# Router logits from four column tiles, and the second sum over states moved ahead of them

## The chip, the cores and the metric

The kernel runs on one NeuronCore of a Trainium2 chip. The metric is the device time of one execution in microseconds; a lower time is better. The time before is the median of three runs, the profile is of a fourth execution.

## The reference, cut to what matters

The reference is one transformer-like layer on x of shape (4, 2048, 256): an adaLN-modulated Mamba block (selective scan), then an adaLN-modulated mixture of experts with 8 experts, of which one is shared and one of the other seven is chosen for each token.

```python
h = layernorm(x) * (1 + ca) + sa
x = x + ga * mamba(h)          # in_proj, conv of 4 taps, silu, x_proj, dt_proj, softplus,
                               # scan of 16 states over 2048 steps, * silu(res), out_proj
h = layernorm(x) * (1 + cb) + sb
x = x + gb * moe(h)

def moe(x_MD):                 # D = 256, H = 512, N = 8 experts, the last one shared
    s_raw_MN = x_MD @ Wg_DN    # the router's logits: (8192, 256) @ (256, 8)
    routed = softmax(s_raw_MN[:, :7])
    sel = routed * one_hot(top_1(routed))
    gates = [sel / sum(sel), softmax(s_raw_MN[:, 7:])]
    for each expert: y += g[:, None] * ((silu(bgate) * a) @ w2),  a, bgate = split(x_MD @ w1)
```

## The kernel before

The 8192 tokens are worked through as 16 chunks of 512 (T); four chunks make one batch row, after which the scan's state starts anew. All data is float32. The 512 channels times 16 states of the scan are cut into 16 sets (NSET): set s holds 32 channels, and its tile in the ring `hs` has 128 partitions (32 channels by 4 groups of states) by 4 (NG) states by 512 steps. The ring has 8 slots.

For each set the engines do this. ScalarE makes dA with four exponentials, one for each of the set's four scans, into three PSUM banks (L843, `exps`; exponential number u waits for scan u-3). VectorE multiplies u by B into the ring (L954, `states_in`) for ten of the sets, GpSimd for the other six (L1258), and VectorE does four scans per set (L967, `scan_set`). ScalarE saves the last state of each set (L863, `save`); GpSimd waits for that and multiplies the set by C (L1265, `weigh_states`). TensorE sums four sets over the states with `sum_states` (L585), four matmul streams side by side in column tiles of 32; the result y of group j (`SUM`, j) is gated by VectorE (L976). GpSimd's states_in for set 13 waits for the second sum (`y_ready`), since the ring's slot is free only then.

All other work is laid between these steps by tables written out by hand. `plan` lists TensorE's groups of matmuls by set, `evict` and `vector` the steps with which ScalarE and VectorE take their results, by set and by position g after one of the set's four exponentials or scans, `gps` GpSimd's and `transfers` SyncE's. Each engine does its list strictly in order. The second number of an entry is the offset of its chunk: in the body of chunk c the front of chunk c+1 or c+2 is made (`T`, `XS`, `CV`, `RS`, `XP`, `DT`, `DB`), and the back of chunk c-1: `OP` (out_proj), `T2` (transposes of the second norm), `RB` (transposes back into rows, for the store to `token_rows`), `GL` (the router's logits), `A` and `B` (the shared expert's two halves), `Y` (its second matmul).

Results of TensorE that ScalarE takes go alternately to two PSUM banks, in the order of `plan` (`bank_of`: the index among ScalarE's groups modulo 2); those that VectorE takes go to a third. `take_bank` lets a group start only when the bank's former content was taken.

Around the change, in set 9 of `plan`: `GL` multiplies 128 tokens at a time (stationary, 128x128) with the router's weights (moving, 8 columns), for 4 tiles of tokens by 2 halves of D (L550). Then comes `RB` 1 (four transposes, L545), then `SUM` 1 (L585), then `B` 0 to 3 (L556). ScalarE copies the logits into `lg` (L734) in set 10 behind the first exponential, then takes two logarithms (L742) and the transposes (L730); it copies `B` 0 behind the third, `B` 1 behind the fourth exponential of set 10, `B` 2 behind the last of set 11, `B` 3 behind the first of set 12 (L738). Behind the second exponential of set 12 comes `SRS`: a table load, silu of the next chunk's `res` (L750), silu of the shared expert's gate (L754), a table load (L757). VectorE gates `SUM` 1 behind the second scan of set 10. SyncE stores the rows (L385) once `RB` 1 is copied; behind that in its queue are the loads of d_rep for set 12 and later (L365).

A sum over states and the logits as they are:

```python
for n in range(NG):                      # SUM, L583 to L587
    for q in range(SPC):
        last = nc.tensor.matmul(ps_[DS * q:DS * q + DS, :], t["gather"], hs[:, (SPC * j + q) % RING, n, :],
                                start=(n == 0), stop=(n == NG - 1), skip_group_check=True, tile_position=(0, DS * q))
```

When the 16 chunks are done, the tokens are sorted to their experts, and the routed experts run for 70 tiles of tokens, from about 2028 us to the end.

## Time and profile before

| what | value |
|---|---|
| median of three runs | 2469.89 us (2469.07 to 2472.47) |
| the profiled execution's own time | 2472.81 us |
| its span, first to last instruction | 2471.1 us |
| mean granted TensorE clock | 0.905 |
| TensorE busy | 2179.9 us, 88% |
| VectorE busy | 1946.6 us, 79% |
| GpSimd busy | 1981.0 us, 80% |
| ScalarE busy | 1344.0 us, 54% |

The profiled execution took 1.7 us more than its span, and 2.9 us more than the median. In the views, PE is TensorE, PEld its weight loads, DVE VectorE, ACT ScalarE, POOL GpSimd, SPq SyncE's DMA queue. A float32 matmul has two records (two passes) in the trace, a transpose one. The granted clock is given as a share of 2.4 GHz, so 0.5 is 1.2 GHz. "<-" names the instruction that ended an engine's idle time.

### The profile page before, as it was taken

Reading aid. Unit: us, or ns where it says so; the run is one execution under the profiler, and the core shown is the slowest. Engines: PE = TensorE matmul, PEld = TensorE weight load, DVE = VectorE, ACT = ScalarE, POOL = GpSimd, SP = SyncE. Lnnn points to the kernel's source line nnn. Section 1 sums busy time; section 2 is a strip of 40 time slices with the busy share of each in tenths; the row PEclk is TensorE's granted clock in tenths of the full one; section 3 lists DMA queues with packets and bytes.
Section 4 is the critical chain, followed back from the end, with each engine's and each line's share of the span. In section 5 each row is a group of like instructions: output and inputs, shape, how many; then the busy total and the mean of one; then the engine's idle time right before and its main releaser. Section 6 shows DMA issues by size and latency. Waiting matters only on the chain. (4 is left out here: it accounts for less than half of the span.)

```text
span 2471.1 us, 31167 instructions
## 1 busy us (share of the span) xinstructions
PE 2179.9 (88%) x7668; PEld 1057.8 (43%) x7669; DVE 1946.6 (79%) x2106; ACT 1344.0 (54%) x2377; POOL 1981.0 (80%) x858
## 2 busy tenths in 40 slices
PE   8759999989989898989898989998975679999998
PEld 3214343434434343434343444343432455565665
DVE  2799898999999999989999999999999852222222
ACT  3666666666675757576666666666655212222221
POOL 1999898899989898989898989889889554555553
PEclk9868888898989898989898989989887889999999
DMA  5444242424242423333324324342322512222221
GB/s 156 134 112 98 66 99 77 100 67 112 80 100 66 104 71 98 81 98 83 98 70 99 91 74 120 86 101 68 92 71 60 192 51 82 86 85 85 87 85 47
DMA packets 148362, 224.37 MB, mean 91 GB/s; under 512 B 47187, under 2 KB 84577, under 8 KB 144098
## 3 DMA queue, kind: packets, MB, share of 16 engines
q1 hardware_dynamic: 134818, 182.40, 28.2%
q0 software_dynamic: 13376, 40.12, 5.3%
q8 instruction: 57, 0.93, 0.2%
q14 instruction: 111, 0.91, 0.1%
HBM read 99.46 MB, written 31.45 MB: 53 GB/s over the span
## 5 line engine op out<-in xcount | busy, mean ns | idle before, releaser
L1265 POOL TENSOR_TENSOR ring<-ring,reps 128x2048 f32<-128x2048 f32 x256 | 1154.5, 4529 | 41.4 <-ACT state L863 41.3
L967 DVE TENSOR_TENSOR_SCAN ring<-dA,state,ring 128x512 f32<-128x512 f32 x768 | 930.9, 1263 | 20.5 <-ACT dA L843 16.3
L843 ACT ACTIVATE dA<-d_rep,a 128x512 f32<-128x512 f32 x1024 | 689.7, 686 | 426.9 <-DVE ring L967 423.2
L1258 POOL TENSOR_TENSOR ring<-u_rep,reps 128x2048 f32<-128x2048 f32 x96 | 436.3, 4545 | 90.2 <-PE bank L585 90.2
L954 DVE TENSOR_TENSOR ring<-u_ps,reps 128x2048 f32<-128x2048 f32 x160 | 360.7, 2271 | 11.1 <-PE u_ps L575 5.7
L556 PE MATMUL bank<-n,w1s 128*128 128x512 f32 x512 | 268.3, 661 | 63.5 <-DVE delta L935 39.2
L585 PE MATMUL bank<-ring,spread 128*32 128x512 f32 x2048 | 285.2, 707 | 31.3 <-POOL ring L1265 26.8
L967 DVE TENSOR_TENSOR_SCAN ring<-dA,ring 128x512 f32<-128x512 f32 x256 | 294.1, 1201 | 20.7 <-ACT dA L843 19.5
L1539 DVE TENSOR_TENSOR hid<-z,sg 128x512 f32<-128x512 f32 x70 | 48.4, 692 | 293.8 <-ACT sg L1516 293.8
L1454 PE MATMUL z<-ring,hT 128*128 x560 | 260.7, 608 | 3.3 <-issue 1.9
L514 PE MATMUL bank<-xin,w_in 128*128 128x512 f32 x512 | 246.3, 621 | 9.1 <-ACT xin L696 9.1
L518 PE MATMUL bank<-xpad,w_conv 128*128 128x512 f32 x512 | 230.7, 600 | 8.3 <-ACT us L711 8.2
L525 PE MATMUL bank<-xdbl,w_dt 65*128 65x512 f32 x256 | 149.8, 683 | 68.5 <-ACT n L727 50.4
L556 PEld LDWEIGHTS bank<-n,w1s 128*128 128x128 f32 x512 | 97.3, 203 | 209.9 <-issue 105.8
L1421 POOL DMA_INDIRECT out<-outr,cur x70 | 71.0, 1014 | 143.3 <-DVE outr L1532 136.3
L575 PE MATMUL u_ps<-us,spread 32*128 32x512 f32 x320 | 165.0, 719 | 2.5 <-DVE ring L954 2.5
L585 PEld LDWEIGHTS bank<-ring,spread 128*32 128x32 f32 x2048 | 69.5, 127 | 225.6 <-issue 206.3
L514 PEld LDWEIGHTS bank<-xin,w_in 128*128 128x128 f32 x512 | 99.7, 198 | 131.6 <-issue 119.9
L1454 PEld LDWEIGHTS z<-ring,hT 128*128 128x128 f32 x560 | 101.4, 191 | 121.1 <-issue 120.9
L518 PEld LDWEIGHTS bank<-xpad,w_conv 128*128 128x128 f32 x512 | 95.1, 190 | 135.5 <-issue 114.7
L1516 ACT ACTIVATE sg<-z 128x512 f32<-128x512 f32 x70 | 41.8, 597 | 197.5 <-PE z L1454 194.7
L1472 PE MATMUL y_ps<-reps,hidT 128*128 x560 | 132.4, 379 | 0.8 <-ACT hidT L1505 0.8
(232 smaller groups left out, 2538.4 us busy)
## 6 DMA issues: line engine op xcount, KB each, us to landing
d_rep<-delta SPq DMA_DIRECT2D x1024, 64.0 KB, 2.0
reps<-bc_rows SPq DMA_DIRECT2D x128, 256.0 KB, 6.1
u_rep<-us SPq DMA_DIRECT2D x384, 64.0 KB, 2.0
xres<-in_x SPq DMA_DIRECT2D x16, 512.0 KB, 3.6
token_rows<-xpad SPq DMA_DIRECT2D x32, 256.0 KB, 2.3
token_rows<-xres SPq DMA_DIRECT2D x16, 512.0 KB, 2.9
xin<-in_x SPq DMA_DIRECT2D x15, 512.0 KB, 9.5
ring<-in_w SPq DMA_DIRECT2D x7, 1024.0 KB, 14.4
```

The lines of the kernel that those rows point to most:

```text
L514: last = nc.tensor.matmul(ps_[:, :], t["w_in"][:, k, col:col + P], hT[:, k, :], start=(k == 0), stop=(k == KD - 1))
L518: last = nc.tensor.matmul(ps_[:, :], t["w_conv"][:, j, k, :], xpad[:, j, k:k + T], start=(k == 0), stop=(k == KCONV - 1))
L525: last = nc.tensor.matmul(ps_[:, :], t["w_dt"][:, j * P:(j + 1) * P], xdbl[0:DT_ROWS, :], start=True, stop=True)
L556: last = nc.tensor.matmul(ps_[:, :], t["w1s"][:, k, col:col + P], h2T[:, k, :], start=(k == 0), stop=(k == KD - 1))
L575: nc.tensor.matmul(u_ps[:, i % 2, :], t["spread"][DS * q:DS * q + DS].rearrange("p f d -> p (f d)"), us[DS * q:DS * q + DS, par, j, :], st ...
L585: last = nc.tensor.matmul(ps_[DS * q:DS * q + DS, :], t["gather"], hs[:, (SPC * j + q) % RING, n, :], start=(n == 0), stop=(n == NG - 1), ...
L843: nc.scalar.activation(dA[:, u % ABANK, :], d_rep[:, q, :], ACT.Exp, scale=t["a"][:, u:u + 1]).then_inc(da_ready, 1)
L954: nc.vector.tensor_tensor(hs[:, s % RING], u_ps[:, i % 2, :].unsqueeze(1).to_broadcast([P, NG, T]), b_rep[:, par, :].rearrange("p (g t) -> ...
L967: nc.vector.tensor_tensor_scan(hs[:, s % RING, g, :], dA[:, u % ABANK, :], hs[:, s % RING, g, :], state[:, u:u + 1] if m else 0.0, ALU.mul ...
L1258: nc.gpsimd.tensor_tensor(hs[:, s % RING], u_rep[:, i % UBUF, :].unsqueeze(1).to_broadcast([P, NG, T]), b_rep[:, par, :].rearrange("p (g t ...
L1265: nc.gpsimd.tensor_tensor(hs[:, s % RING, :, :], hs[:, s % RING, :, :], c_rep[:, par, :].rearrange("p (g t) -> p g t", g=NG), ALU.mult).th ...
L1454: last = nc.tensor.matmul(z[:, q % 2, half, :], hT[:, q % 2, i, :], t["w1r"][:, e, i, half * H:(half + 1) * H], start=(i == 0), stop=(i == ...
```

## The change

The logits are computed the other way round. The router's weights (128x8) become the stationary operand and 128 tokens at a time the moving one; the four tiles of tokens go to four column tiles of the array, and their results to partitions 0, 32, 64 and 96 of a bank. ScalarE copies that (128x128) to SBUF, into the part of `hid` that `B` 1 will fill later (`lgT`). A new group `GT` transposes it in one piece, and ScalarE copies the logits from there into `lg`. `SUM` 1 goes ahead of `GL`; ScalarE's copies of `GL`, `RB` 1, `GT` and `B` 0 to 1 stand later in its list.

```diff
+        lgT = hid[:, 1, 0:P]
@@ plan
-            9: [(('GL', 0), -1), (('RB', 1), -1), (('SUM', 1), 0), (('B', 0), -1), (('B', 1), -1), (('B', 2), -1), (('DB', 0), 1), (('B', 3), -1), (('DT', 2), 1)],
+            9: [(('SUM', 1), 0), (('GL', 0), -1), (('RB', 1), -1), (('GT', 0), -1), (('B', 0), -1), (('B', 1), -1), (('B', 2), -1), (('DB', 0), 1), (('B', 3), -1), (('DT', 2), 1)],
@@ evict
-            10: [[(('GL', 0), -1), (('L0', 0), 1), (('RB', 1), -1)], [], [(('B', 0), -1)], [(('B', 1), -1)]],
-            11: [[], [], [], [(('B', 2), -1)]],
+            10: [[(('L0', 0), 1)], [], [(('GL', 0), -1), (('RB', 1), -1)], [(('GT', 0), -1), (('B', 0), -1)]],
+            11: [[], [(('B', 1), -1)], [], [(('B', 2), -1)]],
@@ TensorE
                 elif kind == "GL":
                     pe.wait_ge(h2T_ready, KD * f + KD)
-                    for tt in range(TT):
-                        for k in range(KD):
-                            last = nc.tensor.matmul(ps_[:, tt * NEXP:(tt + 1) * NEXP], h2T[:, k, tt * P:(tt + 1) * P], t["wg"][:, k, :],
-                                                    start=(k == 0), stop=(k == KD - 1))
+                    for k in range(KD):
+                        for tt in range(TT):
+                            last = nc.tensor.matmul(ps_[DS * tt:DS * tt + NEXP, 0:P], t["wg"][:, k, :], h2T[:, k, tt * P:(tt + 1) * P],
+                                                    start=(k == 0), stop=(k == KD - 1), skip_group_check=True, tile_position=(0, DS * tt))
+                elif kind == "GT":
+                    pe.wait_ge(lgT_ready, f + 1)
+                    last = nc.tensor.transpose(ps_[:, 0:P], lgT, t["ident"][:])
@@ ScalarE
                 elif kind == "GL":
+                    nc.scalar.activation(lgT, ps_[:, 0:P], ACT.Copy).then_inc(lgT_ready, 1)
+                elif kind == "GT":
                     if not (known(f) and f == 0):
                         act.wait_ge(logits_stored, 16 * f)
-                    nc.scalar.activation(lg[:], ps_[:, 0:TT * NEXP].rearrange("p (t e) -> p t e", t=TT), ACT.Copy).then_inc(logits_kept, 1)
+                    nc.scalar.activation(lg[:], ps_[:, 0:P].rearrange("p (t e) -> p t e", t=TT)[:, :, 0:NEXP], ACT.Copy).then_inc(logits_kept, 1)
```

`GT` is one more group among ScalarE's, so from it on `bank_of` gives each group the other of the two banks: `RB` 1 and `B` 0 now use the same bank, with only `GT` between them. In the part after the last chunk, the exponentials of the last chunk's routing stand behind `GT` instead of `B` 0. The orders of VectorE, GpSimd and SyncE are unchanged.

TensorE's order around set 9, from the last matmuls ahead of the logits to the first ones of the shared expert. Before (L575 makes u for a later set, L550 is the logits, L545 `RB` 1, L585 `SUM` 1, L556 `B`):

```order
L575 MATMUL u_ps<-us,spread 128x512
L550 MATMUL bank<-wg,n 128x8 x8
L545 MATMUL bank<-ident,n 128x128 x4
L306 REGISTER_ALU
L582 REGISTER_ALU
L585 MATMUL bank<-ring,spread 32x512 x16
L556 MATMUL bank<-n,w1s 128x512 x4
```

And with the change (here L580, L590, L552, L547, L556 and L561 are u, `SUM` 1, the logits, `RB` 1, `GT` and `B`):

```order
L580 MATMUL u_ps<-us,spread 128x512
L308 REGISTER_ALU
L587 REGISTER_ALU
L590 MATMUL bank<-ring,spread 32x512 x16
L552 MATMUL bank<-n,wg 8x128 x8
L547 MATMUL bank<-ident,n 128x128 x4
L556 MATMUL bank<-ident,xpad 128x128
L561 MATMUL bank<-n,w1s 128x512 x4
```

The sum of 16 matmuls went ahead of the 8 of the logits and the four transposes, and one transpose that waits for ScalarE came between these and `B` 0.

ScalarE's order in set 10. Before (L734 copies the logits, L742 is the logarithm, L730 copies `RB` 1, L738 `B`):

```order
L843 ACTIVATE dA<-d_rep,a 128x512
L734 ACTIVATE lg<-bank 128x32
L742 ACTIVATE delta<-delta 128x1024
L730 ACTIVATE xpad<-bank 128x512
L836 REGISTER_ALU
L843 ACTIVATE dA<-d_rep,a 128x512
L836 REGISTER_ALU
L843 ACTIVATE dA<-d_rep,a 128x512
L310 REGISTER_ALU
L738 ACTIVATE xpad<-bank 128x512
```

With the change, from the third exponential on (L737 copies the column tiles' result, L735 `RB` 1, L741 the logits, L745 `B`):

```order
L850 ACTIVATE dA<-d_rep,a 128x512
L737 ACTIVATE xpad<-bank 128x128
L735 ACTIVATE xpad<-bank 128x512
L869 ISA
L870 ACTIVATE state<-ring 128x4
L843 REGISTER_ALU
L850 ACTIVATE dA<-d_rep,a 128x512
L741 ACTIVATE lg<-bank 128x32
L312 REGISTER_ALU
L745 ACTIVATE xpad<-bank 128x512
```

No copy of a matmul's result stands ahead of the second and third exponential any more, the copy of `RB` 1 moved by two exponentials, and the first copy of `B` by one.

## Rows read from the trace of the kernel before

**Rows 1.** The page: busy us, share of the span, instructions.

```profile
PE 2179.9 (88%) x7668; PEld 1057.8 (43%) x7669; DVE 1946.6 (79%) x2106; ACT 1344.0 (54%) x2377; POOL 1981.0 (80%) x858
```

**Rows 2.** Windows, four steady chunks: PE, PEld, DVE, ACT, POOL busy us (instructions), PEclk, DMA.

```profile
719.00:1179.00 460.00, 417.17 (x1469) 187.22 (x1469) 431.13 (x432) 301.40 (x529) 418.09 (x131) 0.91 0.33 86
```

**Rows 3.** VectorE's waits between 600 and 1520 us: total us, times, longest.

```profile
DVE res L976 <- PE bank L585: 28.8, 12, 3.4
```

**Rows 4.** Timeline of VectorE, the example chunk: start, us, line, op, tiles, [idle <-releaser].

```profile
1193.05 1.28 DVE L967 TENSOR_TENSOR_SCAN ring<-dA,state,ring 128x512 f32<-128x512 f32 x1 [0.60 <-ACT dA L843]
1197.72 0.69 DVE L976 TENSOR_TENSOR res<-bank,res 128x512 f32<-128x512 f32 x1 [3.39 <-PE bank L585]
...
1214.03 2.46 DVE L967 TENSOR_TENSOR_SCAN ring<-dA,state,ring 128x512 f32<-128x512 f32 x2 [0.57 <-ACT dA L843]
```

**Rows 5.** Timeline of TensorE, same chunk.

```profile
1182.33 2.08 PE L525 MATMUL bank<-xdbl,w_dt 65*128 65x512 f32 x2 [2.79 <-ACT n L727]
...
1187.18 3.58 PE L550 MATMUL bank<-wg,n 128*128 128x8 f32 x16
1190.62 1.09 PE L545 MATMUL bank<-ident,n 128*128 128x128 f32 x4
1191.64 6.00 PE L585 MATMUL bank<-ring,spread 128*32 128x512 f32 x32
1197.58 5.42 PE L556 MATMUL bank<-n,w1s 128*128 128x512 f32 x12
...
1218.88 3.64 PE L585 MATMUL bank<-ring,spread 128*32 128x512 f32 x32 [0.71 <-POOL ring L1265]
1222.45 0.66 PE L509 MATMUL bank<-ident,xin 128*128 128x128 f32 x4
```

**Rows 6.** Timeline of GpSimd, same chunk.

```profile
1177.75 13.46 POOL L1265 TENSOR_TENSOR ring<-ring,reps 128x2048 f32<-128x2048 f32 x3
1197.77 4.54 POOL L1258 TENSOR_TENSOR ring<-u_rep,reps 128x2048 f32<-128x2048 f32 x1 [6.55 <-PE bank L585]
```

**Rows 7.** Timeline of ScalarE, same chunk.

```profile
1190.80 0.20 ACT L734 ACTIVATE lg<-bank 128x32 f32<-128x32 f32 x1 [3.35 <-PE bank L550]
...
1205.73 0.58 ACT L738 ACTIVATE xpad<-bank 128x512 f32<-128x512 f32 x1
...
1206.99 1.28 ACT L750 ACT_TABLE_LOAD   x1
...
1213.30 0.69 ACT L843 ACTIVATE dA<-d_rep,a 128x512 f32<-128x512 f32 x1
```

**Rows 8.** Timeline of VectorE, first and last of the 15 waits in set 10.

```profile
255.52 0.69 DVE L976 TENSOR_TENSOR res<-bank,res 128x512 f32<-128x512 f32 x1 [3.51 <-PE bank L585]
...
1898.24 0.69 DVE L976 TENSOR_TENSOR res<-bank,res 128x512 f32<-128x512 f32 x1 [1.58 <-PE bank L585]
```

**Rows 9.** Windows of the example chunk; behind the five busy times stands PEclk.

```profile
1182.80:1196.40 13.60, 13.60 (x52) 6.68 (x55) 10.93 (x9) 7.01 (x14) 8.41 (x2) 0.50 0.59 152
1196.50:1199.90 3.40, 3.40 (x18) 1.25 (x11) 2.00 (x5) 0.30 (x1) 2.13 (x1) 1.00 0.40 101
```

**Rows 10.** Timeline of weight loads inside a sum at full clock.

```profile
1018.26 0.13 PEld L585 LDWEIGHTS bank<-ring,spread 128*32 128x32 f32 x4 [0.30 <-issue]
```

**Rows 11.** Groups of weight loads: busy us, mean ns, idle before.

```profile
L514 PEld LDWEIGHTS bank<-xin,w_in 128*128 128x128 f32 x512 | 99.7, 198 | 131.6 <-issue 119.9 <-ACT xin L696 6.5 <-ACT xpad L701 3.2
...
L585 PEld LDWEIGHTS bank<-ring,spread 128*32 128x32 f32 x2048 | 69.5, 127 | 225.6 <-issue 206.3 <-POOL ring L1265 11.7 <-DVE xres L983 3.4
```

**Rows 12.** Timeline of SyncE's DMA issues, the example chunk.

```profile
1192.67 0.98 SPq L385 DMA_DIRECT2D token_rows<-xpad  x2
1194.01 16.16 SPq L365 DMA_DIRECT2D d_rep<-delta  x16
...
1214.79 2.41 SPq L365 DMA_DIRECT2D d_rep<-delta  x4
```

**Rows 13.** The page's list of DMA issues: count, KB, us from issue to landing.

```profile
d_rep<-delta SPq DMA_DIRECT2D x1024, 64.0 KB, 2.0
```

More of the change, by code:

```diff
@@ L178, in fused_program @@
         logits_made, logits_kept, logits_stored = sem("logits_made"), sem("logits_kept"), sem("logits_stored")
+        lgT_made, lgT_ready = sem("lgT_made"), sem("lgT_ready")
         gate_in, gate_exp, gate_inv, gate_soft, gate_ready = sem("gate_in"), sem("gate_exp"), sem("gate_inv"), sem("gate_soft"), sem("gate_ready")
@@ L259, in fused_program @@
                  ("DT", 0), ("DT", 1), ("DB", 0), ("DT", 2), ("DT", 3), ("DB", 1), ("RS", 0), ("DB", 2), ("RS", 1), ("DB", 3), ("RS", 2), ("RS", 3)]
-        ACT_READS = ("T", "XS", "CV", "RS", "XP", "DT", "T2", "RB", "GL", "B")
+        ACT_READS = ("T", "XS", "CV", "RS", "XP", "DT", "T2", "RB", "GL", "GT", "B")
         made = {"T": turned, "XS": xs_made, "RS": res_made, "CV": conv_made, "XP": xdbl_made, "DT": dt_made, "DB": db_made, "SUM": y_ready, "OP": out_made,
-                "T2": turned2, "RB": back_made, "GL": logits_made, "B": b_made, "A": a_made, "Y": out2_made}
+                "T2": turned2, "RB": back_made, "GL": lgT_made, "GT": logits_made, "B": b_made, "A": a_made, "Y": out2_made}
         kept = {"T": hT_ready, "XS": xs_ready, "RS": res_pre, "CV": us_pre, "XP": xdbl_ready, "DT": exp_ready, "DB": delta_ready, "SUM": yg_ready, "OP": x1_ready,
-                "T2": h2T_ready, "RB": back_kept, "GL": logits_kept, "B": b_kept, "A": hid_ready, "Y": acc_ready}
+                "T2": h2T_ready, "RB": back_kept, "GL": lgT_ready, "GT": logits_kept, "B": b_kept, "A": hid_ready, "Y": acc_ready}
         many = {"T": KD, "XS": KI, "RS": KI, "CV": KI, "XP": 1, "DT": KI, "DB": KI, "SUM": KI, "OP": 2,
-                "T2": KD, "RB": 2, "GL": 1, "B": KI, "A": KI, "Y": 2}
+                "T2": KD, "RB": 2, "GL": 1, "GT": 1, "B": KI, "A": KI, "Y": 2}
         FRONT = ("T", "XS", "CV", "RS", "XP", "DT", "DB")
@@ L896, in _ @@
                     do(item, NCHUNK, 0)
-                    if item[0] == ("B", 0):
+                    if item[0] == ("GT", 0):
                         route_exp(1)
```

## The prediction

> **What bounds the kernel now.** I read the page's busy times first. TensorE, VectorE and GpSimd all look close to full [rows 1], so the share alone names no bound. Four steady chunks show more: VectorE is busy for 431 of 460 us, GpSimd for 418, TensorE for 417, at a granted clock of 0.91 [rows 2]. VectorE has the least idle time, and it is the engine that feeds back (its scans free the banks of ScalarE's exponentials, ScalarE's saves release GpSimd). So whatever makes VectorE wait is the first candidate for the period of a chunk. Its waits name one cause above all: the gate of a sum over states (L976) waited 28.8 us in the eight chunks of that stretch [rows 3].
>
> The timeline of one chunk shows where. VectorE finishes the second scan of set 10, idles 3.39 us, and gates SUM 1 at 1197.72; just before, the scan at 1193.05 had waited 0.60 us for its exponential [rows 4]. The sum is late because TensorE, free at 1187.18, first does the logits (3.58 us) and RB 1 (1.09 us), and starts the sum at 1191.64 [rows 5]. Its input was there: GpSimd did sets 6, 7 and 8 from 1177.75 in 13.46 us, so set 7, the last one the sum needs, ended at about 1186.7, and GpSimd then idled 6.55 us for the sum [rows 6]. The exponential was late since ScalarE took the logits only at 1190.80 [rows 7], and its list has the logarithm and RB 1's copy behind them, ahead of that exponential. The same wait is there in 15 chunks, the first with 3.51 us and the last with 1.58 us, together 42 us [rows 8]; with 0.6 us beside each, the two waits hold 3.4 us per chunk on average, 51 us in all. That is the ceiling of the change.
>
> **The change, part by part.** I count from X = 1187.18, the moment TensorE is free.
>
> 1. The sum first. It took 5.94 us here (1191.64 to 1197.58), and a sum at full clock 3.64 us (the one at 1218.88) [rows 5]. The granted clock was 0.50, that is 1.2 GHz, from 1182.8 to 1196.4 and 1.00 behind that [rows 9]. TensorE had idled 2.79 us before L525 at 1182.33, then did L525, transposes, u and the logits [rows 5]. Moved to X, the sum starts in the same slow stretch. Bounds: 3.6 us if the clock rises at once, 7.3 us if it stays low. I take the 5.94 us it had, since what precedes it (L525, L545, L575) did not lift the clock before either, and the sum did. It ends at X+5.94 = 1193.12. VectorE arrives at 1197.72-3.39-0.60 = 1193.73: the wait of 3.39 us is gone, and so is the 0.60, because no copy of a result stands ahead of the second exponential now. VectorE alone would be 3.99 us earlier.
>
> 2. The logits as column tiles. No row shows a 128x8 weight load with 128 moving columns. There are 16 passes, four at a time. Lower bound: four times the streaming of 128 columns, a quarter of the 0.43 us of 512 [rows 10], 0.4 us. Upper bound: 3.6 us, what the 16 passes take now. A pass of the sum shows four weight loads of 32 columns together in 0.13 us, once every 0.43 us [rows 10]; 4 x (0.13 + 0.11) = 0.96. I take 1.0 us, as the sum has the same tile shape and full overlap of its four streams. Weight loads last 198 ns with 128 columns and 127 with 32 [rows 11]; a line through the two leaves about 0.11 us for 8.
>
>    The Trainium skill (TensorE: Matmul & The Clock Gate, LDWEIGHTS) says a weight load takes its columns divided by 1.2 ns, which would be 7 ns for 8 columns. The rows fall less steeply than that; by the page the logits would take 0.5 us, and the sum below would be 0.5 us per chunk better.
>
> 3. RB 1 and the new round trip. RB 1 at full clock takes 0.66 us (four transposes; at half clock 1.09 [rows 5]; the row at 1222.45 has the same shape at full clock). Meanwhile ScalarE copies the column tiles (between the 0.20 us of 32 columns and the 0.58 of 512 [rows 7], say 0.3) and GT, one transpose of some 0.2 us, runs. These hide behind what comes next: RB 1 and B 0 now share a bank, so B 0 waits for RB 1's copy, 0.60 us plus an estimated 0.1 of signalling. B 0 starts at X + 5.94 + 1.0 + 0.66 + 0.70 = X+8.30 = 1195.48, against 1197.58 now: 2.10 us earlier.
>
> 4. ScalarE's silus. This is the term that decides. B 3's copy started 8.15 us behind B 0 (1205.73), SRS at 1206.99, and the next exponential at 1213.30, 6.3 us later [rows 7]; the scan that needs it started at 1214.03 having waited 0.57 us [rows 4, 7]. With B 0 at 1195.48, B 3's copy comes at 1203.63, SRS at 1204.89, the exponential at 1211.20, the scan at 1211.93: 2.1 us earlier. VectorE would be ready at 1213.46-3.99 = 1209.47, so it now waits about 2.5 us there. Of 3.99 us, 1.9 are given back. Everything behind is released by this scan, by the save after it or by ScalarE's list, and moves by the 2.1 us.
>
> 5. What is queued behind. Behind B 0's copy, now later in ScalarE's list, is the exponential for the fifth scan from the gate: B 0 made at X+10.1, copied by X+10.8, exponential done at X+11.5; VectorE wants it at about X+11.5. No room, no loss. On SyncE the store of rows waits for RB 1's copy, and d_rep for set 12 stands behind it: 1.34 us behind the store, 2.4 us for its four issues [rows 12], 2.0 us to land [rows 13]. The store would go at about 1195.7 instead of 1192.67, so d_rep lands near 1201.4; the exponential that reads it comes at about 1203. Hidden, with 1.6 us left. GpSimd's set 13 starts up to 4 us earlier, then waits for a save behind the silus: no gain. The extra copy and transposition are 0.5 us of ScalarE and TensorE, in waits.
>
> 6. After the last chunk the logits are off the path (VectorE is busy with the earlier tokens' routing): zero, within 1 us. The routed experts from 2028 us on don't change.
>
> **Sum.** 15 chunks x 2.1 = 31 us; I take off 1 for the last one, whose wait is only 1.58 us. From the profiled execution's 2472.8 us this gives 2442.8. Its time was 2.9 us over the median of the runs; against the median the forecast is 2440.
>
> **The rivals.**
>
> *A, nearly the whole ceiling.* The clock rises while the sum is young, since the sum is denser work than what stood in its place. Say it rises 2.4 us into the sum: 2.4 + 2.4 = 4.8 us, and the logits take 0.5. Then B 0 starts at X+6.7, 3.7 us earlier, and 15 x 3.7 = 55 us: 2414. For it: the sum lifted the clock each time. Against: how soon it does is not seen.
>
> *B, another bound at once.* GpSimd's 418 us and TensorE's 417 us of 460 leave under 11 us per chunk, and the sum starts only 0.5 us behind GpSimd's set 7; if GpSimd's chain does not move with the scans, TensorE stands at the sum with the logits behind it, and the period stays. Or d_rep on SyncE runs out of its 1.6 us. Price: all of the 2.1 us, 2469 to 2472.
>
> *C, slower.* The column tiles do not overlap. Then the logits take 16 x (0.127 + 0.107) = 3.7 us, B 0 starts at X+11.0, 0.6 us later than now, and the silus with it: 15 x 0.6 = 9 us, 2479. If the clock also stays low through the sum (7.1 us), it is 1.9 us per chunk, 2498. It decides from 3.1 us of logits on. Against it: weight loads of the sum start every 0.43 us the 0.43 us a pass streams, with no room for a load in between [rows 10].
>
> The Trainium skill (the same page, Part 3: Packing small matmuls, The mechanism) says weight loads overlap running matmuls only in another row group; column tiles share one, so the page speaks for C. By that rule, the trace of the sum disagrees, so C gets little.
>
> *D, it does not do what it says.* The sum is first, yet VectorE still waits because GpSimd's set 7 is late. Then the gain is what is left, some 1 us per chunk: 2455. The forecast's range holds it.
>
> **How the numbers follow.** The forecast with D, 2428 to 2458: 0.60. A: 0.20. B: 0.11. C: 0.09. A measurement of this kernel tells 0.2% (5 us) from no change. Faster by more than that: forecast, D and A, and a little of B, 0.81. Same: most of B, 0.11. Slower: most of C, 0.08. The range of 8 in 10 reaches over most of A to 2415, and to 2467, which leaves out C, half of B and the end of A. The likeliest case's own range is 2428 to 2458.
>
> **What would show it.** Right: SUM 1's start right behind u; L976's wait in set 10 under 0.5 us; ScalarE at SRS 2 us earlier counted from X; the wait of the third scan of set 12 grown from 0.6 to about 2.5 us; logits' 16 records within about 1 us; a chunk's period down by 2.1 us. Wrong: logits records over 2 us, a d_rep landing that ends an exponential's wait, or L976's wait still above 1 us.

## The result and the profile after

The changed kernel takes 2442.22 us, the median of four runs (2440.91 to 2443.93), against 2469.48 us for the kernel before in the same comparison (four runs, 2467.69 to 2472.47). The ratio is 0.9889 with a 95% interval of 0.9872 to 0.9906: 27 us less. The profiled execution took 2443.20 us, its span is 2441.5 us, the mean granted clock 0.917 (0.905 before).

The page of the changed kernel, busy us, share of the span, instructions; it answers to [rows 1]:

```profile
PE 2145.3 (88%) x7684; PEld 1012.7 (41%) x7685; DVE 1945.0 (80%) x2106; ACT 1347.2 (55%) x2393; POOL 1980.6 (81%) x858
```

VectorE and GpSimd do what they did, in a span 30 us shorter. Four steady chunks of the changed kernel, a stretch as long as that of [rows 2]:

```profile
705.00:1165.00 460.00, 415.34 (x1493) 179.74 (x1492) 440.60 (x440) 307.60 (x542) 428.06 (x133) 0.92 0.35 90
```

VectorE stands idle for 19 us of 460 instead of 29. What it still waits for, between 600 and 1520 us (total us, times, longest), against the one cause of 28.8 us in [rows 3]:

```profile
DVE ring L961 <- PE u_ps L580: 9.5, 9, 1.5
DVE res L983 <- PE bank L590: 7.1, 6, 1.4
DVE ring L974 <- ACT dA L850: 6.6, 8, 1.0
```

The gate (now L983) gave back three quarters of its wait. The 28.8 us had two parts: 22.2 were eight waits for the second sum, and 6.6 were four waits for the third one (L976 gates every sum). All 7.1 us that are left are for the third sum. The first row is a wait of a kind that no part of the prediction named: VectorE's product of u for set 12 waits for TensorE's spreading of u.

The chunk that answers to the example chunk, TensorE, where X (TensorE free ahead of the sum) is 1166.73; columns as in [rows 5]:

```profile
1166.73 6.11 PE L590 MATMUL bank<-ring,spread 128*32 128x512 f32 x32
1172.67 0.61 PE L552 MATMUL bank<-n,wg 128*8 128x128 f32 x16
1173.21 0.66 PE L547 MATMUL bank<-ident,n 128*128 128x128 f32 x4
1173.78 0.30 PE L556 MATMUL bank<-ident,xpad 128*128 128x128 f32 x1
1174.55 5.42 PE L561 MATMUL bank<-n,w1s 128*128 128x512 f32 x12 [0.48 <-ACT xpad L735]
...
1183.34 1.12 PE L580 MATMUL u_ps<-us,spread 32*128 32x512 f32 x2
...
1188.92 3.61 PE L561 MATMUL bank<-n,w1s 128*128 128x512 f32 x4 [2.54 <-DVE delta L942]
...
1195.69 5.29 PE L590 MATMUL bank<-ring,spread 128*32 128x512 f32 x32 [0.83 <-POOL ring L1272]
```

The sum starts at X, the 16 passes of logits last 0.61 us (3.58 before), B 0 waits 0.48 us for RB 1's copy (L735) on the shared bank and starts at X+7.82 (X+10.40 before). The last row is the third sum: it was 3.64 us long in [rows 5] and is 5.29 us here.

VectorE in the same chunk:

```profile
1173.09 0.67 DVE L983 TENSOR_TENSOR res<-bank,res 128x512 f32<-128x512 f32 x1
...
1184.50 2.29 DVE L961 TENSOR_TENSOR ring<-u_ps,reps 128x2048 f32<-128x2048 f32 x1 [1.15 <-PE u_ps L580]
...
1190.83 2.46 DVE L974 TENSOR_TENSOR_SCAN ring<-dA,state,ring 128x512 f32<-128x512 f32 x2 [0.77 <-ACT dA L850]
...
1201.05 0.69 DVE L983 TENSOR_TENSOR res<-bank,res 128x512 f32<-128x512 f32 x1 [1.38 <-PE bank L590]
```

The gate stands at X+6.36 without a wait (X+10.54 with 3.39 before), 4.18 us earlier. Then three waits take from it: 1.15 us for u, 0.77 at the scan behind the silus (0.57 before), 1.38 at the gate of the third sum. Before, in the example chunk, the last one was not there. The scan of the second line from the end stands at X+24.10, 2.75 us earlier than the X+26.85 of [rows 4].

ScalarE in the same chunk, answering to [rows 7]:

```profile
1173.35 0.28 ACT L737 ACTIVATE xpad<-bank 128x128 f32<-128x128 f32 x1 [4.00 <-PE bank L552]
1173.90 0.60 ACT L735 ACTIVATE xpad<-bank 128x512 f32<-128x512 f32 x1 [0.27 <-PE bank L547]
...
1182.59 0.60 ACT L745 ACTIVATE xpad<-bank 128x512 f32<-128x512 f32 x1 [1.32 <-PE bank L561]
...
1183.78 1.28 ACT L757 ACT_TABLE_LOAD   x1
...
1190.10 0.69 ACT L850 ACTIVATE dA<-d_rep,a 128x512 f32<-128x512 f32 x1
```

B 3's copy is 8.04 us behind B 0 (8.15 before), the table load 1.19 us behind that, the exponential 6.32 us behind the table load: the chain of the prediction's step 4 kept its length and moved as a whole. One thing in it is new. B 3's copy now waits 1.32 us for TensorE's product of B 3 (L561), 1.15 us in the mean of 14 chunks; before, it waited in none, because ScalarE's own list was just as late. So up to B 3's copy the chain is now TensorE's, where it was ScalarE's, and the two happen to be equally long.

To compare kernels I use one reading throughout. From the timelines of each kernel I took, in the 14 chunks between the first second sum and the fifteenth (from 244 us on), the place of each step counted from that chunk's X, and the length of the chunk (from one X to the next). "Scan behind silus" is the third scan of set 12. Means over the 14, in us; a kernel's name is given by its edit, and the later rows are the experiments below:

| kernel | B 0 at X+ | scan behind silus at X+ | wait, 2nd gate | wait, u of set 12 | wait, that scan | wait, 3rd gate | chunk |
|---|---|---|---|---|---|---|---|
| before | 9.88 | 26.30 | 2.89 | 0.00 | 0.67 | 0.76 | 117.40 |
| the change | 7.58 | 23.85 | 0.03 | 1.05 | 0.84 | 1.05 | 115.23 |
| order alone | 7.99 | 24.23 | 0.00 | 1.24 | 0.85 | 0.45 | 115.36 |
| form alone | 7.09 | 23.36 | 0.71 | 0.00 | 0.67 | 0.97 | 114.50 |
| logits made three times | 8.05 | 24.33 | 0.03 | 1.24 | 0.84 | 0.70 | 115.93 |
| short silu | 7.58 | 22.93 | 0.12 | 0.98 | 0.00 | 0.03 | 113.91 |
| GT on the third bank | 7.42 | 23.68 | 0.12 | 0.67 | 0.90 | 0.96 | 114.88 |
| DT 2 behind u | 7.60 | 23.88 | 0.03 | 0.31 | 1.61 | 1.48 | 115.47 |
| change, more work ahead of the 3rd sum | 7.21 | 23.49 | 0.03 | 0.66 | 0.83 | 0.07 | 114.05 |
| before, the same work | 9.64 | 26.05 | 2.65 | 0.00 | 0.67 | 0.32 | 116.71 |
| form alone, the same work | 6.73 | 23.02 | 0.43 | 0.00 | 0.67 | 0.09 | 113.44 |

From B 0 to the scan it is 16.24 to 16.42 us in every row where the silus are whole. The change brought the scan 2.45 us forward and shortened the chunk by 2.17: 14 x 2.17 = 30.4 us, which is about the difference of the two spans (29.6); the two ends of the kernel, outside these chunks, changed the time by -0.6 and +1.5 us.

### The profile page after: what moved, and what is told of

Same layout as the page of the kernel before. It is cut to its first block and busy times, and to the rows that moved or that the text cites. A ratio compares the mean times of both kernels' runs of the same rounds, so it can differ in the third digit from the quotient of the medians.

```text
span 2441.5 us, 31243 instructions
## 1 busy us (share of the span) xinstructions
PE 2145.3 (88%) x7684; PEld 1012.7 (41%) x7685; DVE 1945.0 (80%) x2106; ACT 1347.2 (55%) x2393; POOL 1980.6 (81%) x858
## 5 line engine op out<-in xcount | busy, mean ns | idle before, releaser
L561 PE MATMUL bank<-n,w1s 128*128 128x512 f32 x512 | 270.1, 665 | 63.2 <-DVE delta L942 34.8
L590 PE MATMUL bank<-ring,spread 128*32 128x512 f32 x2048 | 294.6, 727 | 30.4 <-POOL ring L1272 26.8
L561 PEld LDWEIGHTS bank<-n,w1s 128*128 128x128 f32 x512 | 98.7, 206 | 202.1 <-issue 94.4
L590 PEld LDWEIGHTS bank<-ring,spread 128*32 128x32 f32 x2048 | 71.2, 130 | 249.4 <-issue 214.6
L580 PE MATMUL u_ps<-us,spread 32*128 32x512 f32 x320 | 163.7, 712 | 3.6 <-DVE ring L961 2.5
```

Source lines behind the costliest of these rows:

```text
L561: last = nc.tensor.matmul(ps_[:, :], t["w1s"][:, k, col:col + P], h2T[:, k, :], start=(k == 0), stop=(k == KD - 1))
L580: nc.tensor.matmul(u_ps[:, i % 2, :], t["spread"][DS * q:DS * q + DS].rearrange("p f d -> p (f d)"), us[DS * q:DS * q + DS, par, j, :], st ...
```

## The experiments

Each kernel was timed against the kernel before on the same chip. In these comparisons the kernel before took 2471.85, 2469.93, 2470.42 and 2468.78 us. The theory I started with is step 4 of the prediction: what stands ahead of B 0 on TensorE decides, by way of ScalarE's silus; VectorE's freedom at the second gate is worth nothing beyond that. Its rivals were that the gate's wait itself is what counts, that some other engine is the bound, and, once the profile after was there, that the time is lost again at u or at the third sum.

### The order alone

The kernel before, with its logits as they were, and only the order of the change. ScalarE's copies stand at the places of the change too; of the edit, TensorE's part:

```diff
-9: [(('GL', 0), -1), (('RB', 1), -1), (('SUM', 1), 0), (('B', 0), -1), (('B', 1), -1), (('B', 2), -1), (('DB', 0), 1), (('B', 3), -1), (('DT', 2), 1)],
+9: [(('SUM', 1), 0), (('GL', 0), -1), (('RB', 1), -1), (('B', 0), -1), (('B', 1), -1), (('B', 2), -1), (('DB', 0), 1), (('B', 3), -1), (('DT', 2), 1)],
```

> The kernel before with the order of the change alone: the second sum ahead of logits and RB 1, ScalarE's copies later, the logits in their old form. Theory (B 3's copy lets ScalarE start its silus, and the start of B 0 sets that): VectorE's wait at the sum's gate, 2.8 us per chunk, goes, but the old logits (about 3.4 us) still stand ahead of B 0, which starts at about X+10.0 instead of X+10.4; the third scan of set 12 then waits 3 to 4 us instead of 0.57. Gain 0.4 us per chunk, about 2464 us. Rival (the wait at the gate is what the change removes, and its order does it): 30 us of gain, 2440.

Measured: 2444.52 us (2443.42 to 2445.96), ratio 0.9892 (0.9877 to 0.9907), the same as the whole change. My expectation of about 2464 was wrong, and the time is near the rival's 2440. This run alone can't tell the two apart, as B 0 came 1.89 us earlier in the mean as well; the form alone, below, can. TensorE in one chunk of it:

```profile
1165.75 5.95 PE L585 MATMUL bank<-ring,spread 128*32 128x512 f32 x32
1171.63 1.95 PE L550 MATMUL bank<-wg,n 128*128 128x8 f32 x16
1173.44 0.63 PE L545 MATMUL bank<-ident,n 128*128 128x128 f32 x4
1173.91 5.38 PE L556 MATMUL bank<-n,w1s 128*128 128x512 f32 x12
```

The logits of the old form take 1.95 us here and 3.58 in [rows 5]. The granted clock rises while the sum runs, here 4.70 us into it and in all 14 chunks between 2.4 and 5.7 us, so what stands behind the sum runs at the full one. I had priced the old logits at their half-clock length in both places. The order also saves the bank's wait, since without GT the groups RB 1 and B 0 fall on different banks. One cost the prediction had left 1.6 us of room for shows in this kernel, the load of d_rep behind the stores of rows on SyncE; ScalarE in the same chunk:

```profile
1181.40 0.69 ACT L843 ACTIVATE dA<-d_rep,a 128x512 f32<-128x512 f32 x1 [1.39 <-DMA d_rep<-delta]
```

It stands behind B 2's copy and ahead of B 3's. Such waits are 5.2 us in all, eleven times, and they cost the chain nothing that shows: from B 0 to B 3's copy it is 8.00 us in the mean of 14 chunks here and 8.03 in the change, where the same stretch is spent waiting for B 3's product.

### The form alone

Column tiles, with TensorE's groups and ScalarE's copies in the old order (TensorE's part of the edit):

```diff
-9: [(('SUM', 1), 0), (('GL', 0), -1), (('RB', 1), -1), (('GT', 0), -1), (('B', 0), -1), (('B', 1), -1), (('B', 2), -1), (('DB', 0), 1), (('B', 3), -1), (('DT', 2), 1)],
+9: [(('GL', 0), -1), (('RB', 1), -1), (('SUM', 1), 0), (('GT', 0), -1), (('B', 0), -1), (('B', 1), -1), (('B', 2), -1), (('DB', 0), 1), (('B', 3), -1), (('DT', 2), 1)],
```

> The change with the old order: logits in column tiles, then RB 1, then the second sum, then GT, then B 0; ScalarE's copies where they were, GT's copy ahead of B 0's. Theory: B 0 starts at about X+8, as with the change, since the same work stands ahead of it; VectorE still waits about 1.5 us at the sum's gate, but would have waited behind the silus anyway. 2440 to 2446 us. Rival (the order does it): the gate's wait is only cut by the 2.8 us that the logits lost, and the rest of the gain is missing: 2450 or more.

Measured: 2430.03 us (2428.76 to 2431.02), ratio 0.9831 (0.9818 to 0.9845). That is 12 us less than the whole change: of the two halves of the edit, one makes the other worse. TensorE in one chunk (X = 1159.92):

```profile
1159.92 1.04 PE L552 MATMUL bank<-n,wg 128*8 128x128 f32 x16
1160.90 1.12 PE L547 MATMUL bank<-ident,n 128*128 128x128 f32 x4
1161.94 5.20 PE L590 MATMUL bank<-ring,spread 128*32 128x512 f32 x32
1167.07 0.33 PE L556 MATMUL bank<-ident,xpad 128*128 128x128 f32 x1
1167.24 5.32 PE L561 MATMUL bank<-n,w1s 128*128 128x512 f32 x12
```

Ahead of the sum the logits take 1.04 us and RB 1 1.12, at half clock; behind it they take 0.61 and 0.66. But the sum takes 5.20 us instead of 6.11 (from its start to the next group's, 4.90 against 5.61 in the mean of 14), so the work ahead of GT lasts about as long in either order: in the chunks shown it ends at 7.15 us behind X here and at 7.05 in the change. What differs is the bank. Here ScalarE copies logits and RB 1 while the sum runs, GT and B 0 find their banks free, and B 0 starts at X+7.32 instead of X+7.82. In the means B 0 and the scan are 0.49 us earlier than in the change and the chunk is 0.73 shorter, so the bank is some two thirds of the difference. The profiled executions differ by 13.2 us: 10.2 in the 14 chunks, and 3.1 behind the fifteenth X, of which some 2 lie in the routed experts and have nothing to do with the bank (step 6 below). The second gate waits 0.71 us in the mean. That costs nothing, as the run with the sum between logits and RB 1 shows further down.

### Logits made three times

The eight matmuls of the logits, done three times over with the same result:

```diff
-for k in range(KD):
+for k in list(range(KD)) * 3:
```

> The changed kernel with the eight matmuls of the logits done three times over (the result is the same). Adds 32 records of about 0.04 us, 1.2 us per chunk, ahead of B 0 and behind the sum. Theory: B 0 and with it the silus are 1.2 us later, 15 x 1.2 = 18 us, 2460. Rival (TensorE has slack here now that VectorE no longer waits at the gate): within 4 us of the change, 2442.

Measured: 2450.49 us (2450.08 to 2454.40), ratio 0.9915 (0.9902 to 0.9929), 8.3 us over the change. The logits' record grew from 0.61 to 1.48 us:

```profile
1178.33 1.48 PE L552 MATMUL bank<-n,wg 128*8 128x128 f32 x48
```

Thirty-two more passes cost 0.87 us, 0.11 us for four. That is what 128 columns of a moving operand last at full clock by [rows 10] (a quarter of 0.43), so the loads cost nothing: each hides behind the streams before it. I had expected 1.2 us. B 0 came 0.47 us later in the mean, the chunk grew by 0.70. The sign is the theory's, the size is between its parts: the sum was 0.40 us shorter (5.21 us from its start to the logits', in the mean, against 5.61). The trace shows how: the clock rose 3.56 us into the sum here and 4.38 us into it in the change, and each microsecond at half clock does half the work. Why it rose earlier was not found.

### A shorter silu

The change, with the silu of the shared expert's gate done for 8 of its 2048 columns in the chunks: 0.20 us instead of 1.90, so that 1.7 us of ScalarE's chain behind B 3 are gone. It leaves out the rest of the shared expert's activation. The expectation speaks of a smaller edit than the one that ran, two of four parts and 0.9 us.

```diff
-silu_shared(c - 1)
+nc.scalar.activation(hid[:, :, 0:2], hid[:, :, 0:2], ACT.Silu)
```

> The changed kernel with the silu of the shared expert's gate done for two of its four parts only (the other two stay without it), so ScalarE's stretch of silus is 0.9 us shorter in each chunk. Theory: the third scan of set 12 gets its exponential 0.8 us earlier, its wait of 0.77 us goes: 12 us less, 2430. Rival (the waits for u of set 12 and for the third sum take its place at once): 2440.

Measured: 2420.52 us (2419.97 to 2421.43), ratio 0.9793 (0.9780 to 0.9806), 21.7 us less than the change, where 12 were expected of the smaller edit. The scan behind the silus no longer waits at all. It comes 0.92 us earlier in the mean, hardly more than the 0.84 it had waited: the rest of the 1.7 us is off VectorE's path. The gate of the third sum does not wait either (0.03 us against 1.05). TensorE in one chunk:

```profile
1184.40 3.64 PE L590 MATMUL bank<-ring,spread 128*32 128x512 f32 x32
```

The third sum took 3.6 us in 10 of 14 chunks, in the change in none (there 4.7 to 5.3). The chunk is 1.32 us shorter, more than the scan's 0.92. So ScalarE's chain behind B 3 bounds the chunk, as the theory says, and something the theory did not hold hangs on the third sum.

### GT on the third bank

GT takes VectorE's bank, so that logits, RB 1 and B 0 alternate on ScalarE's two:

```diff
-scalar_items = [g for g, off in items if g[0] not in VECTOR]
+scalar_items = [g for g, off in items if g[0] not in VECTOR + ("GT",)]
```

> The change, with the transposed logits (GT) put in VectorE's bank, so that B 0 no longer follows RB 1's copy on the same bank. Theory of the path (everything ahead of B 0 on TensorE sets ScalarE's silus and scan 50): the wait of 0.48 us ahead of B 0 goes, B 0 at X + 7.3, scan 50 earlier by 0.48 in each of 15 chunks, 7 us in all: 2435. Theory of the u bound (VectorE's wait for set 12's u and the third sum's clock set the end, not B 0): no change, 2442 within 2.

Measured: 2435.49 us (2434.40 to 2437.47), ratio 0.9859 (0.9844 to 0.9874), 6.7 us less than the change. The theory of the path had said 7, from a B 0 that comes 0.48 us earlier. That it fits is mostly luck: the wait of 0.48 us for RB 1's copy is gone, but GT shares its new bank with the sum, and so now waits for the gate:

```profile
1171.35 0.33 PE L556 MATMUL bank<-ident,xpad 128*128 128x128 f32 x1 [1.11 <-DVE res L983]
```

In 9 of 14 chunks B 0 starts at X+7.23 to X+7.28, just behind that gate. In the mean B 0 is only 0.16 us earlier than in the change and the scan 0.17, half of the 0.35 by which the chunk is shorter. So the sign is the theory's and the size isn't shown to be, and no run here takes the bank's wait away and nothing else.

### More work ahead of the third sum

In the change TensorE stands still for 2.54 us ahead of A 0, then does A 0 in 3.61 us, about twice the 1.88 that the same four passes take for B 3. The granted clock in the change from 1172.7 us to 1184.0, and from A 0 to the third sum (the number behind the five busy times):

```profile
1172.70:1184.00 11.30, 10.82 (x47) 4.85 (x39) 10.38 (x17) 7.76 (x17) 10.51 (x7) 1.00 0.35 100
...
1188.90:1195.60 6.70, 5.32 (x10) 1.88 (x10) 5.93 (x6) 6.69 (x13) 4.50 (x2) 0.75 0.35 82
```

The experiment fills the gap with work that writes the same numbers again:

```diff
+for _ in range(5 if g == ("DT", 3) and off == 1 else 1):
...
-for k in range(KD):
+for k in list(range(KD)) * (2 if g == ("A", 0) else 1):
```

> The change, with DT 3's product made five times and A 0's twice over (same numbers written again), so that TensorE doesn't stand still for 2.5 us ahead of A 0 and the third sum. Theory of the clock (the third sum's 5.29 us at half clock against 3.64 at full clock take back 1.4 us a chunk at the gate): the third sum takes 3.64, the gate wait behind it goes, 15 x 1.2 = 18 us: 2424. Rival (the gate's wait is bound by when the third sum starts, by GpSimd's set 11, so the clock is worth nothing, and the added work costs what it lasts): 2442 to 2455.

Measured: 2432.12 us (2431.42 to 2436.22), ratio 0.9851 (0.9836 to 0.9866), 10 us less with more work done. TensorE and VectorE in one chunk of it:

```profile
1177.31 5.42 PE L528 MATMUL bank<-xdbl,w_dt 65*128 65x512 f32 x12
1182.57 3.60 PE L562 MATMUL bank<-n,w1s 128*128 128x512 f32 x8
...
1188.62 3.64 PE L591 MATMUL bank<-ring,spread 128*32 128x512 f32 x32 [0.82 <-POOL ring L1273]
```

```profile
1193.00 0.67 DVE L984 TENSOR_TENSOR res<-bank,res 128x512 f32<-128x512 f32 x1
```

A 0's eight passes now last what its four did, the third sum is 3.64 us in 13 of 14 chunks, and its gate does not wait. In the 14 chunks the kernel is 16.5 us shorter than the change (14 x 1.18); 5 us of it are paid back ahead of the first chunk, where X comes at 249.27 instead of 244.23 us. Not all of the 1.18 us is the third sum's, though: the second sum is 0.30 us shorter too (5.31 against 5.61), and B 0 and the scan behind the silus come 0.36 us earlier with it. So the clock theory holds, in both places, and its size of 18 us was nearly met in the chunks and missed in the whole.

### The same work in the kernel before

The kernel before, with DT 3's product made five times and A 0's twice over:

> The kernel before, with DT 3's product made five times and A 0's twice over, as in the run that took the change from 2442 to 2432. Theory of a loss that both kernels have (in the kernel before six of fourteen third sums already ran over 4.9 us and the gate behind them waited 0.76 us in the mean of fourteen chunks): 10 us less, 2460 within 3, and third sums of 3.64. Rival (only the change pushes the third sum into the half clock): 2468 to 2472.

Measured: 2467.89 us against 2468.78, ratio 0.9998 (0.9989 to 1.0007): no difference that can be measured, where the theory had 10 us. I had left out what the work costs ahead of the first chunk: 3.6 us (X at 248.42 instead of 244.86). In the 14 chunks of the profiled execution the kernel is 9.7 us shorter (14 x 0.69), the third gate's wait is down from 0.76 to 0.32 us, and the third sum takes 3.6 us in 10 of 14 chunks instead of 7; the span is 5.6 us shorter (2465.5), of which the medians show 1. So the rival's number came, but in the chunks the theory's mechanism is there. Of the 0.69 us a chunk, 0.25 is the scan behind the silus coming earlier, as the second sum is shorter here too. Both kernels lose something to the clock, and the change loses more: 16.5 against 9.7 us in the 14 chunks, second and third sum together.

### Late copies

TensorE's order of the form alone, ScalarE's table as in the change.

```diff
-10: [[(('GL', 0), -1), (('L0', 0), 1), (('RB', 1), -1)], [], [(('GT', 0), -1), (('B', 0), -1)], [(('B', 1), -1)]],
-11: [[], [], [], [(('B', 2), -1)]],
+10: [[(('L0', 0), 1)], [], [(('GL', 0), -1), (('RB', 1), -1)], [(('GT', 0), -1), (('B', 0), -1)]],
+11: [[], [(('B', 1), -1)], [], [(('B', 2), -1)]],
```

> TensorE's order of the kernel that took 2430 (logits, RB 1, then the second sum), but ScalarE's copies at the late places of the change. If ScalarE's places decide (RB 1's copy late, and B 0 on its bank): B 0 at X + 7.8 or later and the gate's wait of 0.9 on top, 2442 to 2455. If only TensorE's order decides: 2430 within 3.

Measured: 2430.59 us (2428.85 to 2431.12), ratio 0.9840 (0.9826 to 0.9853), as the form alone. The places turned out not to be late at all, ScalarE being there in time:

```profile
1161.63 0.26 ACT L737 ACTIVATE xpad<-bank 128x128 f32<-128x128 f32 x1
1161.78 0.59 ACT L735 ACTIVATE xpad<-bank 128x512 f32<-128x512 f32 x1
```

With X at 1159.07, RB 1 is copied by X+3.3, while the sum runs. The two tables differ little in time; it is TensorE's order that sets the copy behind the sum.

### Logits, then the sum, then RB 1

The column tiles first, the sum in the middle, RB 1 behind it, GT on the third bank, and ScalarE's copy of the logits at its early place. TensorE's part of the edit:

```diff
-9: [(('SUM', 1), 0), (('GL', 0), -1), (('RB', 1), -1), (('GT', 0), -1), (('B', 0), -1), (('B', 1), -1), (('B', 2), -1), (('DB', 0), 1), (('B', 3), -1), (('DT', 2), 1)],
+9: [(('GL', 0), -1), (('SUM', 1), 0), (('RB', 1), -1), (('GT', 0), -1), (('B', 0), -1), (('B', 1), -1), (('B', 2), -1), (('DB', 0), 1), (('B', 3), -1), (('DT', 2), 1)],
```

> Column-tile logits first (copied early), then the second sum, then RB 1, and B 0 on a bank of its own. The sum starts at X + 1.0 instead of X + 2.0 and B 0 keeps X + 7.3. Theory of the path: the gate wait of 0.9 becomes about 0.1, but scan 50 waits on B 0's chain, so only what scan 50 had spare (nothing, it waits 0.57 already) counts: 2430 within 4, with a longer wait at scan 50 (about 1.3) and perhaps at u for set 12. Rival (the two halves add, 27 us for the order and 40 for the form): 2418 or less.

Measured: 2435.16 us (2434.61 to 2438.33), ratio 0.9862 (0.9847 to 0.9877). The sum starts a microsecond earlier than in the form alone, the second gate waits 0.07 instead of 0.71 us, and the kernel is 5 us slower. An earlier sum is worth nothing by itself; u and the scan behind the silus take it back (0.61 and 0.84 us), and B 0 is 0.18 us later in the mean, for the wait of GT that the run with GT on the third bank had too. The halves do not add.

### DT 2 behind u

DT 2's product moved out of the way of u for set 12:

```diff
-9: [(('SUM', 1), 0), (('GL', 0), -1), (('RB', 1), -1), (('GT', 0), -1), (('B', 0), -1), (('B', 1), -1), (('B', 2), -1), (('DB', 0), 1), (('B', 3), -1), (('DT', 2), 1)],
-10: [],
+9: [(('SUM', 1), 0), (('GL', 0), -1), (('RB', 1), -1), (('GT', 0), -1), (('B', 0), -1), (('B', 1), -1), (('B', 2), -1), (('DB', 0), 1), (('B', 3), -1)],
+10: [(('DT', 2), 1)],
```

> The change, with DT 2's product moved behind the spreading of u for set 12, so that TensorE has that u earlier and most of VectorE's new wait for it (1.15 us in the chunk shown) goes. Theory of the path (scan 50 waits 0.77 us behind it on an exponential that stands behind ScalarE's silus): what VectorE gets back at the u it waits at scan 50, no gain, 2442 within 3. Rival (the u wait is where the lost time sits): 0.6 to 1.2 us a chunk, 2424 to 2433.

Measured: 2444.55 us (2442.27 to 2446.14), ratio 0.9895 (0.9880 to 0.9910): no gain. The wait for u fell from 1.05 to 0.31 us and the one at the scan rose from 0.84 to 1.61, by about as much. VectorE in one chunk:

```profile
1191.29 2.46 DVE L974 TENSOR_TENSOR_SCAN ring<-dA,state,ring 128x512 f32<-128x512 f32 x2 [1.19 <-ACT dA L850]
```

So the largest wait of VectorE in the profile after costs nothing. It lies ahead of one that would take its place.

### Form alone with the work ahead of the third sum

The form alone, with the edit of "more work ahead of the third sum":

> The kernel that took 2430 (column tiles in the old order) with DT 3's product made five times and A 0's twice over, the edit that took the change from 2442 to 2432. Theory of two separate losses (B 0's start, and the third sum's clock): they add; its gate waits of some 1.4 us in two of three chunks go, 10 us less, 2420 within 3. Rival (the two share one path, so one hides the other): 2428 to 2431.

Measured: 2419.40 us (2417.82 to 2421.56), ratio 0.9797 (0.9783 to 0.9810), the fastest kernel with the whole computation. It is 10.6 us under the form alone, as the same work took 10.1 from the change, so the two losses add. The third sum of one chunk:

```profile
1301.80 3.64 PE L591 MATMUL bank<-ring,spread 128*32 128x512 f32 x32 [0.83 <-POOL ring L1273]
```

### B 3 ahead of DB 0

The kernel of the last run, and:

```diff
-(('B', 2), -1), (('DB', 0), 1), (('B', 3), -1)
+(('B', 2), -1), (('B', 3), -1), (('DB', 0), 1)
```

> As the run before, and B 3 ahead of DB 0 on TensorE. Theory of the path (ScalarE stands waiting only ahead of the copies of B 0 and B 1, and from there to the silus works without a gap): B 3 made 1 us earlier is worth nothing, within 2 us of the run before. Rival (B 3's product releases the silus): 0.5 to 1.0 us a chunk, 8 to 15 us less.

Measured: 2425.06 us (2419.28 to 2427.00), ratio 0.9815 (0.9801 to 0.9828), with runs that scatter more than any other kernel's. In its steady chunks the timelines are those of the run before to 0.1 us; one early chunk of the profiled execution is 120.15 us long where it had been 115.66. That is no gain, as expected, and a loss of 5.7 us, where I had allowed 2. The trace of the early chunk shows where most of it went: DT 3's twelve passes ran at half clock.

```profile
266.07 10.32 PE L528 MATMUL bank<-xdbl,w_dt 65*128 65x512 f32 x12
```

In the run before they took 5.42 us in that chunk. Why the clock fell there was not found. In this order of TensorE, B 3's product does not release the silus; ScalarE's own list from B 0 on does. That can't be carried over to the change itself, where ScalarE waits 1.15 us for B 3's product: there, B 3 ahead of DB 0 could gain, and was not tried.

## Why the prediction was right, and where it was not

The forecast was 2440 and the median is 2442.22; against the profiled execution 2442.8 was forecast and 2443.20 came. The cause was right too. That the number came so close is luck: the logits were priced too dear and the second sum a little too long, and against that stand the third sum and the start of the routed experts, which were not priced.

- **Step 1, the sum.** I took 5.94 us from its start to the next group's, and the example chunk has just that (1166.73 to 1172.67); the mean of 14 is 5.61. In two chunks it was 4.7 us, with the clock rising 2.5 and 2.6 us into it, which is the course of rival A. The waits of 3.39 and 0.60 went as said: the second gate waits 0.03 us in the mean.
- **Step 2, the logits.** I took 1.0 us and they take 0.54 (1172.67 to 1173.21). The term that failed is the 0.13 us of weight loads added to each four passes: the thrice-made logits show 0.11 us for four, streams alone. The prediction's 0.5 us by the Trainium skill (TensorE: Matmul & The Clock Gate, LDWEIGHTS) was the better number, yet not for its reason. By the page's rule a load of 8 columns is an estimated 7 ns; the group of these loads has 92 ns in the mean, near the 0.11 us of my line through [rows 11]. They are hidden, so their length is not in the sum.

```profile
L552 PEld LDWEIGHTS bank<-n,wg 128*8 128x8 f32 x256 | 6.6, 92 | 10.6 <-issue 10.2
```

- **Step 3, RB 1 and the bank.** RB 1 takes 0.57 us to GT's start where I had 0.66, and from there to B 0 it is 0.77 where I had 0.70, 0.48 of it a wait for RB 1's copy. Steps 1 to 3 gave X+8.30, the chunk has X+7.82, and nearly all of the 0.48 between them is step 2.
- **Step 4, the silus.** The chain from B 0 to the scan is 16.28 us, 16.45 before. This carried the forecast, and the short silu and the DT 2 run confirm it. (What stands behind B 0 in that chain has changed, as said above: B 3's copy waits for TensorE, and the prediction had not seen that.) The scan stands 2.75 us earlier here and 2.45 in the mean where I had 2.10. The wait of 2.5 us that I foretold for it came as 1.15 us for u and 0.77 behind that. I had not looked at u: with VectorE earlier and B 0 to B 3 still ahead of it on TensorE, u is late next.
- **Not in the sum at all: the third sum.** I had everything behind the scan move with it. The gate of the third sum waits 1.05 us in the mean where it had waited 0.76, as the third sum is at half clock more often. That is the gap between 2.45 us of scan and 2.17 of chunk. My step 4 read one chunk, the example chunk, in which the third sum had run at 3.64; in 7 of the 14 chunks before it took 5.2 us or more. The row was true and not typical.
- **Step 5, the queues.** GpSimd gained nothing, as said: between 240 and 1900 us its wait for a sum fell from 86.7 to 28.0 us and the one for a save rose from 37.3 to 66.0. SyncE's d_rep ended no wait in the example chunk of the change, but did in the order alone (1.39 us), so the room of 1.6 us was as thin as it looked.
- **Step 6, after the last chunk.** I had zero within 1 us and routed experts that don't change. From the fifteenth X to the end it is 582.6 us before and 584.1 now. The last scan is 2.46 us nearer to that X than before, so the fifteenth chunk did gain, and the start of the routed experts lost some 3.5 us of it again: the granted clock is 0.50 from 2004.6 to 2011.4 us, and one group of the experts' first product is at half clock, where it took 3.70 us before.

```profile
2006.28 6.24 PE L1461 MATMUL z<-ring,hT 128*128 x8
```

- **The rivals.** C needed logits of 3.1 us or more. By the Trainium skill (the same page, Part 3: Packing small matmuls, The mechanism) loads overlap only in another row group, and four column tiles share one; the section also names a background buffer for weights, with which a load can be pulled ahead too. By the first rule C would hold, and this trace disagrees: 16 passes last 0.61 us, and those of the thrice-made logits take no longer than their streams. B would have shown no gain. D had VectorE waiting for set 7; the second gate does not wait.

What no part of the prediction asked is whether both halves are needed. The form alone gives 42 us, the order alone 27, and both give 27. The order takes the copies of logits and RB 1 from under the sum, where they were free, and puts one of them ahead of B 0; what it wins at the gate is not on the path. The last is shown by the runs; that the bank is what the order costs is argued from the 0.48 us of wait in the trace, and covers two thirds of the difference in the chunks.

Open are why the clock rose earlier with logits made three times, why it fell in the early chunk of the last run and at the start of the routed experts, and what B 3 ahead of DB 0 would do in the change.

## What to carry to other kernels

When a wait is removed, walk on from it on the same engine to the next wait that other engines set: only what moves that one counts. Here it was mainly ScalarE's silus, which follow B 0, and behind them the third sum. The best edit was the one that shortened what stands ahead of B 0 and left the copies under the sum. A step's length belongs to its place when the clock changes, and a term at the far end of the kernel can change with it; before pricing a move, look at how long that instruction lasts at both clocks, and read several chunks, not one. And when an edit has two halves, count each alone: their gains here were 42, 27 and, together, 27 us.

## What the hardware showed that I had not expected

- The logits of the old form, 16 passes with a 128-column load each and 8 moving columns, take 3.58 us at half clock and 1.95 at full.
- Work repeated for nothing made the kernel faster: 2.54 us of TensorE idle ahead of A 0 go with a granted clock of 0.75 behind it, A 0 at 3.61 instead of 1.88 us and a third sum of 5.29 instead of 3.64. With 5.4 us of DT 3 and a doubled A 0 in that place, the mean granted clock of the kernel is 0.938 (0.917) and it takes 10 us less. In the kernel before, the same work raised the mean granted clock from 0.908 to 0.926 and gained nothing that can be measured.
- Column tiles of 8 columns overlap fully: four passes of 128 moving columns cost 0.11 us at full clock.
